# The subtraction that makes the low half of o moves from GpSimd to VectorE, one unit later

## The chip, the cores and the metric

The kernel runs on one core of one Trainium2 chip. The metric is the device time of one execution in microseconds. Engines are TensorE (PE, with PEld for its weight loads), VectorE (DVE), ScalarE (ACT), GpSimd (POOL) and SyncE (SP), which here only issues DMAs. The engines run their own instruction streams in order, and wait for each other on semaphores.

## The reference, cut to what matters

```python
x = x + xattn(layernorm(x), ctx)      # 16 heads of 16, 64 keys a batch, x is 4 x 1024 x 256
x = x + moe(layernorm(x))             # shared expert, and 2 of 8 experts a token

# inside xattn
attn = clip(q @ k.T * scale, -CLAMP, CLAMP)
p = softmax(attn)
o = p @ v                             # 4096 x 256 for all heads
return o @ Wo + bo
```

Products run in float16, each float32 operand as a sum of two halves: high = float16(a), low = float16(a - high). So each product's operands are split first. This holds for the softmax weights p, for o (ahead of the product with Wo) and for the weights of the experts. The change is about the low half of o.

## The kernel before, in words

Stages follow each other: layer norm, queries and row maxima (to about 133 us of the span), the attention units (133.9 to 256.3 us), the shared expert with routing, the experts chosen per token. The change lies in the attention units.

There are `NU` = 16 units of 256 tokens, with indices u = 0 to 15, and a loop (`run_units`) that calls each engine's `unit(u)` for u = 0 to 20. In one call an engine works on several units at once: `known(u, lag)` says whether u - lag is a unit. The text calls the call for u "unit u", and writes v for the unit whose data is worked on. In unit u:

- TensorE makes the scores of unit u in four PSUM banks (24 matmuls); then for r = 0 to 3 it multiplies p of unit u-2 with the values (`weigh`, 12 matmuls) and subtracts the row maximum from bank r (`subtract_max`, 2 matmuls). Last is `project(u - 4)`, o times Wo, 12 matmuls of 256 columns. The next unit's scores wait until ScalarE has taken the exponentials out of the banks.
- VectorE clips each of the four banks (`clip`, line 932), which `subtract_max` of the same r waits for. Then come, for v = u-5, the residual sum (line 969) and the moments of the second layer norm (lines 976, 982), and for v = u-2 `normalise` (lines 939, 947), which divides by the row sum and writes o in float32 (`o_f`). In units 16 to 18 it also splits weights of the shared expert (`split_lo`, line 989).
- ScalarE takes four exponentials (line 757), casts r = 0 to 2 to the high half of p (line 764), casts `o_f` of v = u-2 to the high half of o (line 777, semaphore `oh_ready`), and casts r = 3. In units 16 to 18 it casts weights (`split_hi`, line 750).
- GpSimd makes the low half of p for r = 0 to 3 (line 608), which `weigh` waits for two units later. Ahead of r = 3 it makes the low half of o for v = u-2 (line 601): it waits for `oh_ready`, and for the transposes that read the buffer two units ago (`ot_got`), and raises `ol_ready`.
- SyncE waits for `ol_ready` and issues two DMA transposes per unit (line 452), which `project(v)` waits for (`ot_got`). `project(v)` also waits for the residual sum of v-1, since they share a bank. `normalise(v)` waits for `ol_ready` of v-2, and ScalarE's cast of o for `ot_got` of v-2.

`o_f`, `o_hl` and `o_t` have two buffers each. The order within each engine is the order in which the code is written.

Of the kernel before, what the change touches and what calls it, by code (L numbers as in the profile page):

```python
# [5 lines left out]
ALU = mybir.AluOpType  # L6
# [11 lines left out]
def build(nc, x, ctx_t, wq, bq, wk, bk, wv, bv, wo, bo, gate_t, w_all, out):  # L18
# [15 lines left out]
    UT = 2  # L34
# [29 lines left out]
    with ExitStack() as ctx:  # L64
# [3 lines left out]
        def sem(name):  # L68
            return ctx.enter_context(nc.semaphore(name))
# [45 lines left out]
        def carve(shape, dt, parts=P):  # L115
            n = 1
            for s in shape:
                n *= s
            cols = n * (2 if dt in (F32, I32) else 1)
            a = arena[0:parts, used[0]:used[0] + cols]  # L120
            used[0] += (cols + 15) // 16 * 16
            assert used[0] <= E * 3 * 2 * 1024
            if dt != F16:
                a = a.bitcast(dt)
            if len(shape) == 1:
                return a
            names = "abcde"[:len(shape)]
            return a.rearrange(f"p ({' '.join(names)}) -> p {' '.join(names)}",
                               **{k: v for k, v in zip(names, shape)})
# [54 lines left out]
        o_f = carve([2, UT, C], F32)  # L184
        o_t = carve([2, UT, 2, HF, P], F16)
        used[0] = loads_from
        o_hl = carve([2, UT, 2, C], F16)
# [97 lines left out]
        oh_ready = sem("oh_ready")  # L285
        ol_ready = sem("ol_ready")
        ot_got = [sem("ot_got0"), sem("ot_got1")]
# [104 lines left out]
        def known(u, lag):  # L392

            return 0 <= u - lag < NU
# [103 lines left out]
        def _(pool):  # L498
# [94 lines left out]

            def unit(u):
                for r in range(RT):
                    if r == 3 and known(u, 2):
                        v = u - 2
                        pool.wait_ge(oh_ready, v + 1)
                        if v >= 2:
                            pool.wait_ge(ot_got[v % 2], 16 * UT * (v // 2))  # L600
                        pool.tensor_tensor(o_hl[:, v % 2, :, 1], o_f[:, v % 2], o_hl[:, v % 2, :, 0],  # L601
                                           ALU.subtract).then_inc(ol_ready, 1)
                    if known(u, 0):
                        k = RT * u + r
                        pool.wait_ge(ph_ready, k + 1)
                        if u >= PB:
                            pool.wait_ge(pv_ready, u - PB + 1)
                        pool.tensor_tensor(p_l[:, u % PB, r], p_f[:, k % FB], p_h[:, u % PB, r],  # L608
                                           ALU.subtract).then_inc(pl_ready, 1)

            run_units(unit)


# [240 lines left out]
        def _(dve):  # L854
# [51 lines left out]
            for n in range(NG):  # L906
# [6 lines left out]
                if n == 6:  # L913
                    dve.wait_ge(v_copied, B)
                    link(dve.tensor_copy(v_hh, v_f))
                    for h2 in range(2):
                        r = slice(h2 * KV, (h2 + 1) * KV)
# [11 lines left out]
            def clip(u, r):  # L929
                if known(u, 0):  # L930
                    dve.wait_ge(st_scored, RT * u + r + 1)
                    dve.tensor_scalar(bank[r][:, :], bank[r][:, :], CLIP, -CLIP, ALU.min,
                                      ALU.max).then_inc(st_clipped, 1)

            def normalise(v):

                dve.wait_ge(pv_ready, v + 1)
                for t in range(UT):
                    ins = dve.reciprocal(r_sum[:, t].rearrange("p (j h) -> p j h", h=2),
                                         bank[4 + t][:, 0:HD // 2 * OW].rearrange(  # L940
                                             "p (j w) -> p j w", w=OW)[:, :, 2 * D:OW])
                ins.then_inc(norm_link, 1)
                dve.wait_ge(norm_link, v + 1)
                if v >= 2:
                    dve.wait_ge(ol_ready, v - 1)
                for t in range(UT):
                    ins = dve.tensor_tensor(
                        o_f[:, v % 2, t].rearrange("p (j h d) -> p j h d", j=HD // 2, h=2),
                        bank[4 + t][:, 0:HD // 2 * OW].rearrange("p (j w) -> p j w", w=OW)
                        [:, :, 0:2 * D].rearrange("p j (h d) -> p j h d", h=2),  # L950
                        r_sum[:, t].rearrange("p (j h) -> p j h", h=2).unsqueeze(3)
                        .to_broadcast([P, HD // 2, 2, D]), ALU.mult)
                ins.then_inc(of_ready, 1)
# [9 lines left out]
            def residual(v):  # L963

                dve.wait_ge(y_ready, v + 1)
                if v == 0:
                    dve.wait_ge(bo_added, NG)
                xu = x_sb[:, bass.ts(v, UT), :]
                dve.tensor_tensor(xu, xu, bank[6][:, :].rearrange("p (t c) -> p t c", t=UT),
                                  ALU.add).then_inc(y_added, 1)  # L970

            def moments(v):

                dve.wait_ge(y_added, v + 1)
                for t in range(UT):
                    link2(dve.bn_stats(stats[:, v % 2, t], x_sb[:, UT * v + t, :]), False)

            def mean_and_variance(v):

                dve.wait_ge(ln2_link, UT * (2 * v + 1))  # L980
                for t in range(UT):
                    link2(dve.bn_aggr(mv2[:, UT * v + t], stats[:, v % 2, t]), False)

            def split_lo(q):

                if q % 2 == 0:
                    w = w_sh[:, q] if q < 3 else w_qs[:, q - 3]
                    dve.wait_ge(w_hi, q + 1)
                    dve.tensor_tensor(w[:, 1], w_stage[:, q % 4, :], w[:, 0], ALU.subtract).then_inc(w_lo[q % 4], 1)

            def unit(u):
                for r in range(RT):
                    clip(u, r)
                if known(u, 5):
                    residual(u - 5)
                    moments(u - 5)
                    mean_and_variance(u - 5)
                if known(u, 2):
                    normalise(u - 2)
                if NU <= u < NU + 3:  # L1000
                    split_lo(u - NU)

            run_units(unit)

            dve.wait_ge(ln2_link, 2 * NT)
# [638 lines left out]
```

## Time and profile before

| | us |
|---|---|
| median of 3 runs | 772.41 (771.75 to 775.31) |
| profiled execution, its own time | 772.33 |
| its span | 770.3 |

| engine | busy us | share of the span |
|---|---|---|
| PE | 623.3 | 81% |
| DVE | 453.0 | 59% |
| POOL | 390.4 | 51% |
| ACT | 347.6 | 45% |

Shares are means over stages with different limits. In the attention units from 182.4 to 201.4 us, for instance, PE, DVE, ACT and POOL are each busy over 90% of the time. The granted clock of TensorE is given as a part of full speed: 1.00 is 2.4 GHz, 0.50 is 1.2 GHz, and a number between them is a mean over a stretch that has both. In a timeline row the columns are the start in us from the start of the span, the duration of the group of instructions merged in the row, the engine, the line of the program, the operation, the tiles written and read with their shapes, the count, and in brackets the idle time of the engine before it with what ended it.

### The profile page before, as it was taken

How to read it: one execution, taken by the hardware profiler on the slowest of the kernel's cores; microseconds unless marked ns; L12 is line 12 of the kernel's file. 1: busy time of each engine (PE TensorE's matmuls, PEld its weight loads, DVE VectorE, ACT ScalarE, POOL GpSimd, SP SyncE). 2: the span in 40 equal slices, each digit the busy share in tenths (PEclk: the TensorE clock that was granted, in tenths of full speed). 3: DMA queues.
4: the chain of work that ended last, by engine and by line, in shares of the span. 5: the costliest groups of instructions: out<-in, count | busy, mean ns of one | idle time of the engine just before them, and what ended most of it. 6: DMA issues, size and time to landing. Idle time of an engine off the chain costs nothing.

```text
span 770.3 us, 15425 instructions
## 1 busy us (share of the span) xinstructions
PE 623.3 (81%) x5262; PEld 419.9 (55%) x5262; DVE 453.0 (59%) x908; ACT 347.6 (45%) x565; POOL 390.4 (51%) x326
## 2 busy tenths in 40 slices
PE   4377855799996187765769989999999999999991
PEld 2134322356564144432445557788787787887881
DVE  5963487557797345667986664444444444544541
ACT  3645661778894365642115434333333333433430
POOL 6738491588996011220002634647566666566643
PEclk9877796558897699987989999999999999999996
DMA  8400000021323438663003556655565565685743
GB/s 265 141 2 0 1 1 0 1 43 34 53 41 60 121 81 197 159 215 73 8 1 110 185 177 112 97 84 99 92 112 92 97 104 88 96 103 90 101 63 34
DMA packets 108170, 66.12 MB, mean 86 GB/s; under 512 B 82946, under 2 KB 101316, under 8 KB 108100
## 3 DMA queue, kind: packets, MB, share of 16 engines
q1 hardware_dynamic: 93268, 41.91, 24.3%
q0 software_dynamic: 14832, 23.24, 18.1%
q8 instruction: 48, 0.79, 0.5%
q14 instruction: 22, 0.18, 0.1%
HBM read 29.47 MB, written 17.96 MB: 62 GB/s over the span
## 4 chain that ended last, share of the span: by engine, by line
PE 52%; DVE 17%; POOL 9%; issue 8%; ACT 7%; DMA 4%; SPq 2%; POOLq 0%; ACTq 0%; DVEq 0%
PE bank L1275 50%; POOL arena L608 5%; POOL arena L601 2%; DVE hidden L1210 2%; SPq L462 2%; DMA out<-w_stage,map_i 1%; ACT arena L691 1%; PE bank L1577 1%; DVE arena L866 1%; PE bank L1333 1%; DMA arena<-arena 1%; ACT arena L792 1%; DVE arena L897 1%; DVE arena L1150 1%; DVE hidden L1177 1%
## 5 line engine op out<-in xcount | busy, mean ns | idle before, releaser
L1275 PE MATMUL bank<-arena 128*128 128x34 f16 (+6 forms) x1284 | 140.9, 255 | 39.1 <-DVE arena L1153 8.8
L1275 PE MATMUL bank<-qx,arena 128*128 128x256 f16 (+1 forms) x1584 | 156.8, 285 | 4.0 <-ACT hidden L757 3.1
L632 POOL DMA_INDIRECT out<-w_stage,map_i x71 | 114.0, 1606 | 74.4 <-DMA out<-w_stage,map_i 36.6
L1275 PEld LDWEIGHTS bank<-qx,arena 128*128 (+1 forms) x1584 | 125.8, 101 | 26.3 <-ACT hidden L757 5.0
L1275 PEld LDWEIGHTS bank<-arena 128*128 128x128 f16 (+2 forms) x1284 | 76.1, 108 | 95.6 <-issue 41.5
L645 POOL TENSOR_TENSOR arena<-w_stage,arena 128x1024 f16<-128x1024 f32 x12 | 26.5, 2206 | 165.9 <-ACT arena L750 165.9
L1244 DVE TENSOR_TENSOR hidden<-bank,hidden 128x512 f32<-128x512 f32 x71 | 49.1, 692 | 104.1 <-ACT hidden L835 104.1
L1275 PE MATMUL bank<-arena,qx 128*128 (+1 forms) x316 | 85.3, 394 | 27.5 <-DVE arena L897 24.7
L1275 PE MATMUL bank<-arena,w_stage 128*128 x852 | 104.6, 273 | 0.6 <-DVE w_stage L1263 0.4
L835 ACT ACTIVATE hidden<-bank 128x512 f32<-128x512 f32 x71 | 42.4, 597 | 127.7 <-PE bank L1275 127.7
L619 POOL DMA_INDIRECT qx<-rows_d,map_i x71 | 71.4, 1006 | 48.5 <-DVE lane_w L1236 30.6
L1275 PE MATMUL bank<-qx,w_sh 128*128 128x512 f16 x384 | 93.6, 396 | 0.0
L1275 PEld LDWEIGHTS bank<-arena,w_stage 128*128 128x128 f16 x852 | 82.3, 98 | 16.9 <-issue 2.9
L608 POOL TENSOR_TENSOR arena<-hidden,arena 128x512 f16<-128x512 f32 x64 | 72.4, 1162 | 28.2 <-ACT arena L764 28.2
L1263 DVE TENSOR_TENSOR w_stage<-hidden,w_stage 128x512 f16<-128x512 f32 x71 | 49.3, 694 | 45.1 <-ACT w_stage L847 45.1
L1275 PE MATMUL bank<-w_sh,hidden 128*128 128x256 f16 x384 | 53.7, 296 | 27.0 <-DVE hidden L1210 27.0
L1275 PEld LDWEIGHTS bank<-arena,qx 128*128 128x128 f16 x316 | 31.1, 100 | 69.8 <-issue 42.7
L1275 PEld LDWEIGHTS bank<-qx,w_sh 128*128 128x128 f16 x384 | 39.3, 102 | 43.3 <-issue 7.3
L897 DVE TENSOR_REDUCE arena<-bank 128x8 f32<-128x512 f32 x64 | 42.4, 688 | 34.6 <-PE bank L1275 34.5
L1275 PEld LDWEIGHTS bank<-w_sh,hidden 128*128 128x128 f16 x384 | 38.9, 105 | 41.1 <-DVE hidden L1210 32.8
L847 ACT CAST w_stage<-hidden 128x512 f16<-128x512 f32 x71 | 43.9, 619 | 37.9 <-DVE hidden L1244 35.6
L806 ACT ACTIVATE hidden<-bank 128x512 f32<-128x512 f32 x32 | 19.1, 596 | 81.4 <-PE bank L1275 81.4
(183 smaller groups left out, 758.8 us busy)
## 6 DMA issues: line engine op xcount, KB each, us to landing
w_stage<-in_w_all SPq DMA_DIRECT2D x27, 512.0 KB, 4.6
x_sb<-in_x SPq DMA_DIRECT2D x8, 512.0 KB, 8.0
rows_d<-arena SPq DMA_DIRECT2D x8, 512.0 KB, 3.5
out<-x_sb POOLq DMA_DIRECT2D x8, 512.0 KB, 5.7
qx<-rows_d,map_i POOLq DMA_INDIRECT x71, 2.9
qx<-qx SPq DMA_TRANSPOSE x71, 2.6
out<-w_stage,map_i POOLq DMA_INDIRECT x71, 3.9
arena<-arena SPq DMA_TRANSPOSE x32, 2.5
```

What stands on the lines that cost most here:

```text
L462: sp.dma_start_transpose(qx[:, :, :, bass.ts(GT * g + t, P)].rearrange("p s h t -> p (s h) t"), x2_hl[:, g % XB, t].rearrange("p a c -> p ...
L608: pool.tensor_tensor(p_l[:, u % PB, r], p_f[:, k % FB], p_h[:, u % PB, r], ALU.subtract).then_inc(pl_ready, 1)
L619: pool.indirect_dma_start(out=gathered(r), out_offset=None, in_=rows_d, in_offset=bass.IndirectOffsetOnAxis(ap=map_i[:, 0, i:i + 1], axis= ...
L632: pool.indirect_dma_start(out=out, out_offset=bass.IndirectOffsetOnAxis(ap=map_i[:, 1, i:i + 1], axis=0), in_=y_sb[:, r], in_offset=None, ...
L645: pool.tensor_tensor(w[:, 1], w_stage[:, q % 4, :], w[:, 0], ALU.subtract).then_inc(w_lo[q % 4], 1)
L806: act.activation(act_g[:, hc % 2], bank[hc % 2][:, :], ACT.Silu).then_inc(silu_ready, 1)
L835: act.activation(act_g[:, k % 2], bank[k % 2][:, :], ACT.Silu).then_inc(sp_silu, 1)
L847: act.copy(h_sp[:, k % 3, 0], h_f[:, k % 2]).then_inc(sp_hh, 1)
L897: dve.tensor_reduce(m_raw[:, n % 2, i, bass.ts(hf, HH)], bank[4 + hf][:, :].rearrange("p (h k) -> p h k", h=HH), AX.X, ALU.max).then_inc(s ...
L1244: dve.tensor_tensor(h_f[:, k % 2], bank[2 + k % 2][:, :], act_g[:, k % 2], ALU.mult).then_inc(sp_h, 1)
L1263: dve.tensor_tensor(h_sp[:, k % 3, 1], h_f[:, k % 2], h_sp[:, k % 3, 0], ALU.subtract).then_inc(sp_hl, 1)
L1275: return pe.matmul(o, a, b, start=first, stop=last, skip_group_check=not check)
```

## The change: what it does

GpSimd no longer makes the low half of o. VectorE makes it, in the same form, in unit u for v = u-3, between the clips of r = 1 and r = 2. The waits move with it. In units 16 to 18, which have no clips, it stands ahead of the residual sum.

```diff
--- before.py
+++ after.py
@@ gpsimd: unit(u) @@
                 for r in range(RT):
-                    if r == 3 and known(u, 2):
-                        v = u - 2
-                        pool.wait_ge(oh_ready, v + 1)
-                        if v >= 2:
-                            pool.wait_ge(ot_got[v % 2], 16 * UT * (v // 2))
-                        pool.tensor_tensor(o_hl[:, v % 2, :, 1], o_f[:, v % 2], o_hl[:, v % 2, :, 0],
-                                           ALU.subtract).then_inc(ol_ready, 1)
                     if known(u, 0):
@@ vector @@
+            def split_o(v):
+
+                dve.wait_ge(oh_ready, v + 1)
+                if v >= 2:
+                    dve.wait_ge(ot_got[v % 2], 16 * UT * (v // 2))
+                dve.tensor_tensor(o_hl[:, v % 2, :, 1], o_f[:, v % 2], o_hl[:, v % 2, :, 0],
+                                  ALU.subtract).then_inc(ol_ready, 1)
+
             def unit(u):
                 for r in range(RT):
                     clip(u, r)
+                    if r == 1 and known(u, 3):
+                        split_o(u - 3)
                 if known(u, 5):
                     residual(u - 5)
                     moments(u - 5)
```

## Rows read from the trace of the kernel before

**Rows 1.** The chain of waits, shares by line, from 145 to 236 us.

```profile
by line: POOL arena L608 44.0%; issue 28.5%; POOL arena L601 15.9%; PE bank L1275 5.6%; DMA arena<-arena 4.5%; SPq L452 1.3%; DVE bank L932 0.8%; ACT hidden L757 0.8%; ACT arena L764 0.6%; POOLq L607 0.4%; POOLq L600 0.2%
```

**Rows 2.** Busy time by stretch: length, each engine's busy us, granted clock, DMA.

```profile
182.40:201.40 19.00, 17.72 (x320) 12.08 (x320) 17.66 (x44) 17.80 (x30) 17.84 (x17) 1.00 0.29 44
201.40:211.70 10.30, 9.91 (x110) 5.96 (x112) 7.13 (x22) 8.29 (x16) 8.73 (x9) 0.67 0.39 54
```

**Rows 3.** Timeline of unit 8, all engines, a unit at the full clock.

```profile
187.25 2.49 DVE L932 TENSOR_SCALAR bank<-bank 128x512 f32<-128x512 f32 x4 [0.31 <-PE bank L1275]
...
188.01 3.96 PE L1275 MATMUL bank<-arena 32*128 32x256 f16 x56 [0.38 <-DVE bank L932]
...
188.43 2.84 ACT L757 ACTIVATE hidden<-bank,arena 128x512 f32<-128x512 f32 x4
189.04 0.51 PEld L1275 LDWEIGHTS bank<-arena 128*128 128x128 f16 x14 [0.21 <-issue]
189.65 0.68 DVE L969 TENSOR_TENSOR x_sb<-x_sb,bank 128x512 f32<-128x512 f32 x1
...
189.76 0.51 PEld L1275 LDWEIGHTS bank<-arena 128*128 128x128 f16 x14 [0.21 <-POOL arena L608]
...
191.17 1.65 ACT L764 CAST arena<-hidden 128x512 f16<-128x512 f32 x3
...
191.69 0.76 DVE L947 TENSOR_TENSOR arena<-bank,arena 128x256 f32<-128x256 f32 x2
...
192.72 0.62 ACT L777 CAST arena<-arena 128x512 f16<-128x512 f32 x1
```

**Rows 4.** Timeline of DVE and of POOL: first clips and first subtractions of units 5, 7, 8, 9.

```profile
167.67 2.49 DVE L932 TENSOR_SCALAR bank<-bank 128x512 f32<-128x512 f32 x4 [3.21 <-PE bank L1275]
...
181.75 2.49 DVE L932 TENSOR_SCALAR bank<-bank 128x512 f32<-128x512 f32 x4 [1.81 <-PE bank L1275]
...
192.76 2.49 DVE L932 TENSOR_SCALAR bank<-bank 128x512 f32<-128x512 f32 x4 [0.32 <-PE bank L1275]
...
165.10 3.38 POOL L608 TENSOR_TENSOR arena<-hidden,arena 128x512 f16<-128x512 f32 x3 [0.99 <-ACT arena L764]
...
179.58 3.38 POOL L608 TENSOR_TENSOR arena<-hidden,arena 128x512 f16<-128x512 f32 x3 [1.55 <-ACT arena L764]
...
186.35 3.39 POOL L608 TENSOR_TENSOR arena<-hidden,arena 128x512 f16<-128x512 f32 x3 [1.16 <-ACT arena L764]
```

**Rows 5.** VectorE subtractions of this shape, with GpSimd idle (min/median/max ns) and busy.

```profile
L1263 DVE TENSOR_TENSOR w_stage<-hidden,w_stage x71: 681/693/748, 464.6 to 752.3; 128x512 f16<-128x512 f32 x71
...
298.06 2.12 POOL L645 TENSOR_TENSOR arena<-w_stage,arena 128x1024 f16<-128x1024 f32 x1 [11.54 <-ACT arena L750]
298.53 2.20 DVE L1210 TENSOR_TENSOR hidden<-hidden 128x512 f16<-128x512 f32 x1 [1.57 <-ACT hidden L820]
...
109.05 2.89 POOL L565 TENSOR_TENSOR qx<-arena,qx 128x512 f16<-128x512 f32 x2
109.40 1.52 DVE L912 TENSOR_TENSOR arena<-arena 128x512 f16<-128x512 f32 x1
```

**Rows 6.** Timeline of PEld: the 12 weight loads of `project` at either clock.

```profile
196.07 1.21 PEld L1275 LDWEIGHTS bank<-arena 128*128 128x128 f16 x12 [0.30 <-DMA arena<-arena]
...
201.69 2.26 PEld L1275 LDWEIGHTS bank<-arena 128*128 128x128 f16 x12 [0.33 <-issue]
```

**Rows 7.** Timeline of units 15 to 20, all engines.

```profile
228.97 2.49 DVE L932 TENSOR_SCALAR bank<-bank 128x512 f32<-128x512 f32 x4 [0.32 <-PE bank L1275]
...
238.15 0.62 ACT L777 CAST arena<-arena 128x512 f16<-128x512 f32 x1 [2.57 <-DMA arena<-arena]
...
239.75 1.84 DVE L989 TENSOR_TENSOR w_sh<-w_stage,w_sh 128x1024 f16<-128x1024 f32 x1 [1.97 <-ACT w_sh L750]
...
245.03 1.16 POOL L601 TENSOR_TENSOR arena<-arena 128x512 f16<-128x512 f32 x1 [4.52 <-ACT arena L777]
...
251.60 0.69 DVE L969 TENSOR_TENSOR x_sb<-x_sb,bank 128x512 f32<-128x512 f32 x1 [0.58 <-PE bank L1275]
```

## The prediction

> **What bounds the kernel now.** I read the attention stage in four steps. The chain of waits comes first: from 145 to 236 us it gives GpSimd 60% (line 608 with 44.0%, line 601, the one that moves, with 15.9%) [rows 1]. Taken alone this promises a gain of up to 16 times 1.12 us. The busy times by stretch speak against it: between 182.4 and 201.4 us TensorE, VectorE, ScalarE and GpSimd are busy 17.72, 17.66, 17.80 and 17.84 us of 19.00 [rows 2]. Four engines stand at their limit, and the chain had to choose one.
>
> So I went to the timeline of unit 8 [rows 3], whose first clip starts at 187.25; unit 9's starts at 192.76 [rows 4], a period of 5.51 us. Of it ScalarE uses about 5.45 (exponentials from 188.43, casts from 191.17, o from 192.72), so with GpSimd free the floor is ScalarE's, under 0.1 us away. VectorE waits 0.32 us in the period, ahead of the first clip, and works 5.19. TensorE's loop is the tight one: scores, first clip, first `subtract_max` (188.01), three steps of 0.72 us (189.04 to 189.76 is one), `project`, next scores. GpSimd needs 5 times 1.12 = 5.6 us and drifts behind, but what it makes is used two units later. Removing its line 601 shortens no loop by itself, except the 0.30 us for which `project` waits on late transposes [rows 6].
>
> Last, the clock. It is 1.00 from 182.4 to 201.4 us and 0.67 on the mean in the next 10.3 us [rows 2]: some of that at 1.2 GHz. A `project` at the lower clock takes 2.26 us of weight loads, not 1.21 [rows 6]. Scores behind it are slower too. Units that have this take about 7.1 us instead of 5.5. They can be told by how long ahead of the first clip GpSimd starts on p: 2.57 us in unit 5 (165.10 and 167.67), 2.17 in unit 7, 0.90 in unit 8 [rows 3, 4]. Units 5, 6, 7, 11, 12 are of this slow kind (2.17 to 2.57, mean 2.32), units 8, 9, 10, 13, 14 of the fast kind (0.90 to 0.98).
>
> **The change part by part.**
>
> *Removed from GpSimd:* 16 subtractions of 1.16 us (one in [rows 7]). Worth about 0.3 us in all by the reasoning above, the wait of `project`.
>
> *Added to VectorE:* 16 subtractions of 128x512, two inputs from SBUF. With GpSimd idle this form takes 0.69 us (71 rows, 681 to 748 ns), 0.60 from start to start. With GpSimd at work it takes longer, and the rows show how: one starts at 298.53 while GpSimd's runs from 298.06 to 300.18, and ends at 300.73; it takes 2.20 us. One at 109.40 takes 1.52, and the two GpSimd instructions beside it take 2.89 instead of 2.32 [rows 5]. I read this as turns: VectorE gets nothing until GpSimd's current instruction ends, then runs 0.55 us, and GpSimd's next one waits for it.
>
> Two rules of the Trainium skill bear on this, both on "GPSIMD Engine Reference". Its "Engine selection" sends elementwise work on a tile to VectorE as about twice as fast; its "Specifications" says that GpSimd's SBUF interfaces are shared with VectorE, with contention for instructions with two SBUF inputs. By the first alone an added subtraction would cost 0.60 us and this sum would be that of the first rival below; the trace agrees with it only where GpSimd is idle.
>
> *Where the added instruction falls.* In unit 8 clips start every 0.60 us (187.25 to 189.65 for four [rows 3]), so it would start at 188.45. GpSimd's first three subtractions run from 186.35 to 189.74 [rows 4]; the second ends at 188.62. The added one ends at 189.17, and the third clip starts at 189.08 instead of 188.45: 0.63 us late. TensorE would take the third `subtract_max` at 188.01 + 2 x 0.72 = 189.45; the clip for it was there at 189.21. So 0.24 us is hidden and 0.39 is not. What is behind the instruction on VectorE moves by 0.63: clips 2 and 3, residual, moments, `normalise`. That chain then fills the period, 5.19 + 0.63 = 5.82 against TensorE's 5.90. ScalarE's cast of o starts after `normalise` and still ends about 0.5 us before VectorE wants it, so the moved wait on `oh_ready` costs nothing in units 3 to 15. Five fast units: 5 x 0.39 = 2.0 us.
>
> In a slow unit the first clip comes later against GpSimd's p, and the instruction meets the last of the four. Unit 7: start at 181.75 + 1.20 = 182.95; GpSimd's third ends at 182.96 and its fourth follows at once, until 179.58 + 4.5 = 184.1. The third clip then starts at 184.55, 1.6 us late, 1.36 of it visible. Unit 5: 1.2 late, 0.96 visible. The late clips are 3.78 us less the lead, so the five units lose 5 x (3.78 - 2.32 - 0.24) = 6.1 us. In units 3 and 4 the clock is 0.50, TensorE's steps are about 1.0 us, and the 0.6 us is hidden.
>
> *The end of the stage, units 15 to 20,* in us after the first clip of unit 15 (228.97 [rows 7]). Before, GpSimd lags: ScalarE's cast of o(14) starts at 9.2 because it waits for transposes that line 601 released late. After, these are in time, but VectorE is later. In unit 16 the added instruction needs o(13)'s cast, which ends at 6.5, then a turn behind GpSimd, until 7.8; residual, moments and `normalise` of v=14 end at 10.55, and the cast starts at 10.6, 1.4 late. `split_hi` and `split_lo` follow; the latter took 1.84 us beside GpSimd [rows 7] and now takes 1.2: 0.8 late. The added instruction of v=14 makes it 1.4 late again; that of v=15 takes 0.7 where GpSimd's took 1.2. Residuals and weight splits then queue in order, and the last residual (251.60, 22.6) comes at about 23.8. Cost 1.2 us; bounds -1.5 (the transposes' early arrival decides) and +3.2 (all four added instructions are on the path).
>
> *The clock.* The added wait leaves TensorE idle 0.4 to 1.4 us more in each unit, between the steps. No row shows what that does. Bounds: the falls stop (four of them cost 1.6 us each, and their units no longer pay the larger wait, 1.0 each: about -10 us), or every fast unit becomes slow, 5 x (1.6 + 0.85) = +12. I take one more slow unit, +2.4, as in the rows it is the stretches with the least matmul work that are followed by a fall. "TensorE: Matmul & The Clock Gate" of the Trainium skill, section "HAM oscillation", blames falls on long idle gaps; by it the short ones added here would cost nothing and the term would be 0. The trace doesn't agree: the fall at 201.4 us follows 19 us in which TensorE was busy 93%.
>
> *Sum:* 2.0 + 6.1 + 1.2 - 0.3 + 2.4 = 11.4 us. On the profiled execution's 772.33 us, which is 0.1 from the median of 772.41, that gives 783.7. The stages behind only start later. Bounds of the loop alone: at least 10 x 0.36 = 3.6 (never a turn to wait for), at most 10 x (0.60 + 1.12 - 0.24) = 14.8 (a whole GpSimd instruction each time).
>
> **The rivals.**
>
> *The instruction is not stretched in the loop.* The two turns meet well, and it costs 0.60 us everywhere: 10 x 0.36 + 1.2 - 0.3 = 4.5, 776.8 us. For it: in fast units it is nearly so (0.63), and in units 7 and 12 the start misses the end of GpSimd's third instruction by hundredths. Against it: units 5, 6 and 11 miss it by 0.15 us or more.
>
> *The clock stays up: no slower than before.* If the longer period moves `project` so that the falls of units 5 to 7, 11 and 12 don't happen, ten units take 5.9 us each, 59.0 instead of 61.3 (167.67 to 228.97 [rows 4, 7]). With 1.2 for the end and -0.3 it is 771.0 us. It decides from the point where three or more of the five slow units become fast. For it: units 8 to 10 kept the full clock with 0.38 us idle per unit. Against it: the added wait lowers TensorE's share of work, and unit 5 starts from the lower clock.
>
> *The clock falls in nearly every unit.* Slow units are longer, and so have longer stretches without `project`; the state keeps itself up. All ten slow: 9.0 + 12.3 = 21.3 us, 793.6.
>
> **How the numbers follow.** Changes under 0.5% (3.9 us, so 768.5 to 776.3) can hardly be told from none. Forecast (turns, clock much as before, 777 to 790): 0.62, all slower. Not stretched: 0.12, half of it slower by over 0.5%. Clock stays up: 0.11, 0.07 of it the same and 0.04 faster. Clock falls everywhere: 0.15, slower. Faster 0.04, same 0.13, slower 0.83. The range 774.5 to 793 leaves out the steady clock and the upper half of the last case, 0.18 together. The predicted time is 783.7.
>
> **What would show it.** The trace after must have 16 subtractions on VectorE with GpSimd idle after its fourth p of each unit; those of fast units take about 0.7 us, those of slow ones 1.3 to 1.7, each ending 0.55 us behind the end of a GpSimd instruction. TensorE must wait for the third clip in each unit from 5 on, the period of fast units be 5.9 us, and `project` wait for no transposes. The last residual should come 23.8 us after unit 15's first clip. It is wrong if the added instructions take 0.69 us beside a busy GpSimd, if TensorE's steps don't open up, or if the number of `project` groups at 2.26 us is far from six.

## The result, and the profile after

The changed kernel takes 796.41 us (median; 788.68 to 799.09) where the kernel before takes 773.86 us (771.75 to 775.77). The ratio is 1.0276, with a 95% interval of 1.0195 to 1.0356: slower by 2.8%. The interval lies wholly above 1, though not wholly above 1.02. The prediction was 783.7 us with a range of 774.5 to 793: the sign was right, the loss is twice the 11.4 us forecast, and the time lies above the range. The profiled execution took 794.96 us, with a span of 793.0.

In the changed kernel the lines of GpSimd, ScalarE and VectorE up to `clip` stand 7 lower (608 is now 601, 932 is 925, 969 is 962), the added subtraction is line 989, and the matmul helper 1278.

The chain of waits of the changed kernel, by line, from 145 to 252 us (answers to [rows 1]):

```profile
by line: PE bank L1278 63.2%; DVE bank L925 16.5%; DVE arena L989 11.5%; issue 6.5%; ACT hidden L750 1.3%; DVE x_sb L962 1.1%; DVEq L960 0.0%
```

GpSimd, 60% before, is gone from it. TensorE, the clips and the added subtraction are the chain now: the tie of four engines [rows 2] has become, by this chain, a loop of two.

Busy times by stretch, the kernel before and the changed one (columns as in [rows 2]):

```profile
165.00:235.00 70.00, 65.71 (x1027) 42.95 (x1026) 56.00 (x144) 60.18 (x104) 62.75 (x57) 0.87 0.27 43
```

```profile
165.00:235.00 70.00, 59.72 (x754) 35.23 (x753) 51.92 (x116) 43.46 (x74) 36.52 (x33) 0.68 0.16 32
```

In 70 us TensorE does 754 matmuls instead of 1027, and the granted clock is 0.68 on the mean instead of 0.87. So more of the stretch was run at 1.2 GHz.

Unit 7 of the changed kernel, timeline, with the start of unit 8 (answers to [rows 3, 4]):

```profile
177.95 4.50 POOL L601 TENSOR_TENSOR arena<-hidden,arena 128x512 f16<-128x512 f32 x4 [3.81 <-ACT arena L757]
...
180.26 1.30 DVE L925 TENSOR_SCALAR bank<-bank 128x512 f32<-128x512 f32 x2 [1.67 <-PE bank L1278]
...
181.46 1.53 DVE L989 TENSOR_TENSOR arena<-arena 128x512 f16<-128x512 f32 x1
...
182.92 1.28 DVE L925 TENSOR_SCALAR bank<-bank 128x512 f32<-128x512 f32 x2
183.66 0.13 PEld L1278 LDWEIGHTS bank<-arena 32*128 32x128 f16 x2 [1.25 <-DVE bank L925]
...
185.18 2.26 PEld L1278 LDWEIGHTS bank<-arena 128*128 128x128 f16 x12 [0.41 <-issue]
...
189.35 1.30 DVE L925 TENSOR_SCALAR bank<-bank 128x512 f32<-128x512 f32 x2 [2.45 <-PE bank L1278]
```

GpSimd's fourth subtraction ends at 182.45. The added instruction waits for that from 181.46 and ends 0.54 us behind it. The third clip is 1.46 us late, TensorE's weight loads wait 1.25 for it, then `project` runs at 1.2 GHz (2.26 us of weight loads), and the next scores take longer too (weight loads 0.99 us, from 187.85, instead of 0.56 at 2.4 GHz). The unit takes 9.09 us. The added instructions (minimum, median, maximum in ns):

```profile
L989 DVE TENSOR_TENSOR arena<-arena x16: 682/1052/1620, 150.0 to 266.3; 128x512 f16<-128x512 f32 x16
```

**Where the 22.7 us of span are.** First clips and last residual sums give the sum. From the first clip of unit 5 to that of unit 15 it is 84.91 us (163.25 to 248.16) instead of 61.30: +23.6. From there to the last residual sum it is 25.97 instead of 22.63: +3.3. Behind that it is +0.2, and the first clip of unit 0 came at 131.36 instead of 135.43, with units 0 to 5 0.35 shorter: -4.4. The stage ahead isn't touched by the change, and its length moves from run to run (131.4 to 137.4 us in the profiles below). So the units and their end cost 26.9 us in this pair of profiles; between the medians of the whole kernel it is 22.6. Two profiles are not two kernels, however: e8 below has the same program as the changed kernel in units 0 to 14, and from unit 5 to unit 15 it took 79.93 us, 5 us less.

At the end, the last `project` of the changed kernel and that of the kernel before (answers to [rows 7]):

```profile
271.37 2.72 PE L1278 MATMUL bank<-arena 128*128 128x256 f16 x12 [0.87 <-DVE x_sb L962]
```

```profile
250.09 1.47 PE L1275 MATMUL bank<-arena 128*128 128x256 f16 x12 [2.70 <-DMA arena<-arena]
```

The last residual sum follows at 274.13, where it was at 251.60.

### The profile page after: what moved, and what is told of

The parts are those of the page before. It is cut to its first block, busy times and chain, and to the rows that moved or that the text cites. A ratio compares the mean times of both kernels' runs of the same rounds, so it can differ in the third digit from the quotient of the medians.

```text
span 793.0 us, 15425 instructions
## 1 busy us (share of the span) xinstructions
PE 636.8 (80%) x5262; PEld 424.4 (54%) x5262; DVE 467.9 (59%) x924; ACT 347.3 (44%) x565; POOL 375.3 (47%) x310
## 3 DMA queue, kind: packets, MB, share of 16 engines
q1 hardware_dynamic: 93268, 41.91, 22.6%
## 4 chain that ended last, share of the span: by engine, by line
PE 56%; DVE 21%; ACT 8%; issue 6%; DMA 4%; SPq 2%; POOL 2%; another core or an unknown queue 1%; POOLq 0%; ACTq 0%; DVEq 0%
PE bank L1278 54%; DVE bank L925 2%; DMA out<-w_stage,map_i 2%; DVE hidden L1213 2%; DVE arena L989 2%; SPq L462 2%; ACT arena L684 1%; PE bank L1580 1%; DVE arena L859 1%; PE bank L1336 1%; POOL out L625 1%; ACT arena L785 1%; DVE arena L890 1%; DVE arena L1153 1%
## 5 line engine op out<-in xcount | busy, mean ns | idle before, releaser
L1278 PE MATMUL bank<-arena 128*128 128x34 f16 (+6 forms) x1284 | 152.1, 268 | 47.7 <-DVE bank L925 14.8
L1278 PE MATMUL bank<-qx,arena 128*128 128x256 f16 (+1 forms) x1584 | 160.6, 299 | 4.3 <-ACT hidden L750 3.1
L1278 PEld LDWEIGHTS bank<-qx,arena 128*128 (+1 forms) x1584 | 127.6, 105 | 28.4 <-issue 5.8
L1278 PEld LDWEIGHTS bank<-arena 128*128 128x128 f16 (+2 forms) x1284 | 80.2, 112 | 111.3 <-issue 47.5
L828 ACT ACTIVATE hidden<-bank 128x512 f32<-128x512 f32 x71 | 42.4, 597 | 127.8 <-PE bank L1278 110.0
L925 DVE TENSOR_SCALAR bank<-bank 128x512 f32<-128x512 f32 x64 | 41.0, 690 | 36.2 <-PE bank L1278 36.2
L750 ACT ACTIVATE hidden<-bank,arena 128x512 f32<-128x512 f32 x64 | 43.4, 687 | 42.5 <-PE bank L1278 42.0
```

The costliest lines, as they stand in the source:

```text
L750: act.activation(p_f[:, k % FB], bank[r][:, :], ACT.Exp, scale=exp_scale).then_inc(exp_ready, 1)
L828: act.activation(act_g[:, k % 2], bank[k % 2][:, :], ACT.Silu).then_inc(sp_silu, 1)
L1278: return pe.matmul(o, a, b, start=first, stop=last, skip_group_check=not check)
```

## The experiments

Ratios are to the kernel before, run beside each experiment on the same chip; its median there was 771.52 us beside e1 to e4, 774.47 beside e5 to e8 and 774.14 beside e9 to e11. The changed kernel was timed only in the first set (before: 773.86). So experiments are compared with each other and with the changed kernel by the ratios, and a difference counts as shown where the intervals don't overlap. "Units" is the time from unit 5's first clip to unit 15's in the profile, "clock" the mean granted clock from 165 to 235 us, each from one profiled execution. For e7 that was the longest of its four (794.45 us), for e8 the shortest of its five (790.06).

| kernel | median us | ratio, 95% interval | units us | clock |
|---|---|---|---|---|
| before | 773.86 | 1 | 61.30 | 0.87 |
| changed | 796.41 | 1.0276 (1.0195 to 1.0356) | 84.91 | 0.68 |
| e1 one input from PSUM | 788.55 | 1.0254 (1.0194 to 1.0314) | 79.97 | 0.65 |
| e2 behind the clips | 788.34 | 1.0236 (1.0169 to 1.0303) | 78.18 | 0.68 |
| e3 changed, 8 fillers | 784.0 | 1.0169 (1.0106 to 1.0231) | 66.81 | 0.92 |
| e4 GpSimd relieved only | 769.99 | 0.9991 (0.9959 to 1.0024) | 65.73 | 0.82 |
| e5 before, 4 fillers | 769.24 | 0.9922 (0.989 to 0.9955) | 56.13 | 1.00 |
| e6 behind the moments, 4 fillers | 772.41 | 0.9967 (0.9934 to 1.0001) | 60.85 | 0.98 |
| e7 changed, 4 fillers | 788.0 | 1.0146 (1.0079 to 1.0213) | 77.36 | 0.81 |
| e8 end on GpSimd | 797.37 | 1.028 (1.0219 to 1.034) | 79.93 | 0.76 |
| e9 e7 with input from PSUM | 781.2 | 1.008 (1.004 to 1.0121) | 70.13 | 0.83 |
| e10 before, fillers everywhere | 765.94 | 0.9875 (0.9817 to 0.9932) | 59.70 | 0.93 |
| e11 behind the moments | 781.39 | 1.0072 (1.0039 to 1.0105) | 67.68 | 0.79 |

The theory going in: the loss has two parts, the third clip's delay (VectorE's added work and its turns with GpSimd), and the clock, which falls because of it. The rivals were that VectorE's load alone sets the pace, and that the clock falls for another cause.

**e1: the turns taken away.**

```diff
-                dve.tensor_tensor(o_hl[:, v % 2, :, 1], o_f[:, v % 2], o_hl[:, v % 2, :, 0],
+                dve.tensor_tensor(o_hl[:, v % 2, :, 1],
+                                  bank[7][:, 0:C].unsqueeze(1).to_broadcast([P, UT, C]), o_hl[:, v % 2, :, 0],
                                   ALU.subtract).then_inc(ol_ready, 1)
```

> The changed kernel, but the first input of VectorE's added subtraction is read from an idle PSUM bank instead of o_f, so it has one input from SBUF and not two; place, shape, waits and the other input stay. (What it writes as the low half of o is not o's.) Theory 1 (turns: it waits for GpSimd's running instruction because both want SBUF): the 16 instructions take 0.68 us each instead of 0.68 to 1.62, the third clip is 0.6 us late instead of 1.0 to 1.5, and TensorE's wait for it falls from 0.66-1.23 us to about 0.4. At ten units that is 4 to 6 us less; with more, if the clock falls less often: 777 to 792 us. Theory 2 (the added work on VectorE costs it, whatever GpSimd does): 796, as the changed kernel.

All 16 take 0.68 us now:

```profile
L989 DVE TENSOR_TENSOR arena<-bank,arena x16: 678/680/691, 151.3 to 262.1; 128x512 f16<-128x512 f32 x16
```

With one input from SBUF there is no wait for GpSimd, though GpSimd still runs beside it: this is the clean result. TensorE's matmuls wait 0.29 us for the third clip in six of the ten units and not at all in the others (0.12 to 1.23 in the changed kernel). The median lies within what theory 1 expected, at its upper end, but the ratio of 1.0254 can't be told from the changed kernel's 1.0276, and units of 8.0 us are what e8 took with the turns left in. The clock is no better (0.65, with `project` at 2.26 us in all ten units). So while the clock is down, taking the turns away is not shown to be worth any time.

**e2: behind the clips.**

```diff
-                    if r == 1 and known(u, 3):
+                    if r == 3 and known(u, 3):
                         split_o(u - 3)
```

> The changed kernel, but the added subtraction stands behind the clip of r = 3 instead of r = 1, so no clip waits for it. Theory 1 (the cost arises because TensorE waits for the third clip in the middle of its steps, which also lowers the clock in nearly every unit): TensorE has no wait between its steps, the unit takes 5.8 us at the full clock (VectorE's load) and 7.1 with one project at 1.2 GHz, the number of slow projects falls back towards five of ten; 774 to 782 us. Theory 2 (VectorE's load itself sets the pace, wherever the instruction stands): at least 790.

Neither: 788.34, and the ratio (1.0236) can't be told from the changed kernel's. TensorE's steps had no wait for a clip but the first, and the timeline shows one ahead of `project`, in seven of ten units (0.29 to 1.02 us), that I had not thought of:

```profile
205.96 0.68 DVE L962 TENSOR_TENSOR x_sb<-x_sb,bank 128x512 f32<-128x512 f32 x1
...
206.79 2.72 PE L1278 MATMUL bank<-arena 128*128 128x256 f16 x12 [0.53 <-DVE x_sb L962]
```

`project(u - 4)` waits for the residual sum of u-5, which VectorE makes in the same unit behind the clips, and here behind the added subtraction too (from 205.36). Before, that sum ended at 190.33 us in unit 8 [rows 3] and `project`'s weight loads began at 190.48: there were 0.15 us to spare. e11 below is this kernel with the one instruction moved behind the residual sum and the moments, and its ratio is 1.0072, with no overlap.

**e3: more work for TensorE.**

```diff
                     if known(u, 2):
                         weigh(u - 2, r)
+                    if r == 2 and 3 <= u < NU:
+                        for _ in range(8):
+                            mm(bank[7][:, 0:C], ident[:, :], wo_hl[:, 0, 0], True, True)
```

> The changed kernel with 8 more matmuls of 256 columns in each unit from 3 to 15, into an unused PSUM bank, between weigh and subtract_max of r = 2, where TensorE waits 0.66 to 1.23 us for the third clip. They take 0.86 us at 2.4 GHz and 1.7 at 1.2. Theory 1 (most of the loss is the clock, which falls because a stretch without project holds too little matmul work): more work brings less time. The granted clock stays at 1.00 through most of units 5 to 15, project takes 1.2 us instead of 2.26, a unit 6.3 to 6.8 us instead of 8.5: 775 to 785 us. Theory 2 (the clock doesn't answer to such work): 796 or up to 10 us more.

784.0 us, as theory 1 has it: 104 useless matmuls made the attention units shorter, 66.81 us instead of 84.91 (79.93 in e8). The ratio is 1.0169 against 1.0276, with intervals that overlap by a little. From unit 6 on the period is 6.39 us in every unit, with `project` at 1.21 us; in units 3 and 4, where the fillers ran at 1.2 GHz, they cost time (8.3 and 10.1 us instead of 6.6 and 7.9). Here the added instruction takes 0.71 us, as forecast for a fast unit:

```profile
196.19 4.96 POOL L601 TENSOR_TENSOR arena<-hidden,arena 128x512 f16<-128x512 f32 x4 [1.43 <-ACT arena L757]
...
197.09 1.30 DVE L925 TENSOR_SCALAR bank<-bank 128x512 f32<-128x512 f32 x2 [0.57 <-PE bank L1278]
...
198.30 0.71 DVE L989 TENSOR_TENSOR arena<-arena 128x512 f16<-128x512 f32 x1
```

GpSimd starts 0.90 us ahead of the first clip, and its second subtraction ends 0.16 us after the added one starts: 0.16 and 0.55 make the 0.71.

**e4: GpSimd relieved, nothing added.**

```diff
+                        n = C if v < 2 else 16
-                        pool.tensor_tensor(o_hl[:, v % 2, :, 1], o_f[:, v % 2], o_hl[:, v % 2, :, 0],
-                                           ALU.subtract).then_inc(ol_ready, 1)
+                        pool.tensor_tensor(o_hl[:, v % 2, :, 1, 0:n], o_f[:, v % 2, :, 0:n],
+                                           o_hl[:, v % 2, :, 0, 0:n], ALU.subtract).then_inc(ol_ready, 1)
```

> The kernel before, but from the third on GpSimd's subtraction for o covers 16 of 256 columns per tile (the rest of the low half of o is left as it was), with all its waits and signals; nothing is added to VectorE. It shows what the relief of GpSimd is worth alone. My account (four engines at the limit, GpSimd's products are used two units later): 771 to 773.5 us, at most 2 us gained, from transposes that come in time. The chain of waits taken by its shares (GpSimd is the bound): 14 times 1.0 us less, 759 us.

0.9991, with an interval that holds 1: freeing the engine that the chain names with 60% is worth nothing measurable. (The median is 1 us below the 771 to 773.5 expected, as the kernel before beside it was low too, 771.52.) Its fourteen shortened instructions would have given 14 us by the chain. At the full clock the period is 5.51 with it and without it.

**e5: the clock of the kernel before.** The filler in the kernel before, where TensorE waits for the first clip.

```diff
                         weigh(u - 2, r)
+                    if r == 0 and 5 <= u < NU:
+                        for _ in range(4):
+                            mm(bank[7][:, 0:C], ident[:, :], wo_hl[:, 0, 0], True, True)
```

> The kernel before (GpSimd makes the low half of o) with 4 more matmuls of 256 columns in each unit from 5 to 15, into an unused PSUM bank, between weigh and subtract_max of r = 0, where TensorE waits 0.38 us for the first clip. Theory 1 (a stretch without project holds too little matmul work and the clock falls; more work in it holds the clock): all units from 6 on at 5.5 to 5.7 us, none at 7.0; the four or five slow ones give back 1.5 us each, the added work costs at most 0.1 us a unit: 764 to 769 us, faster than before. Theory 2 (the clock's falls have another cause): 771 to 778.

0.9922, faster than before by 0.8%, with an interval below 1; the median is 0.2 us above the range of theory 1, far closer to it than to theory 2. The clock is 1.00 over the whole stretch and nine of ten periods are 5.50 to 5.83 us, the tenth 6.24; none is 7. The 6.24 and the 5.83 are `project` waiting 0.66 and 0.26 us for its transposes: with the clock held, GpSimd's 5.6 us a unit do show, in two units of ten.

```profile
165.00:235.00 70.00, 65.07 (x1165) 45.13 (x1164) 61.92 (x159) 61.04 (x103) 67.99 (x60) 1.00 0.28 46
```

The fillers fill the 0.39 us in which TensorE waited for the first clip. So they add matmul work and take a wait away at once, and which of the two keeps the clock up was not tried apart. Busy time doesn't tell the two kernels apart (65.07 us of 70 here, 65.71 before).

**e6 and e11: behind the moments, with and without the fillers of e5.**

```diff
                     mean_and_variance(u - 5)
+                if known(u, 3):
+                    split_o(u - 3)
                 if known(u, 2):
```

> The changed kernel with the added subtraction moved behind the moments of v = u-5, so that neither a clip nor the residual sum (which project waits for) stands behind it, and with the 4 filler matmuls at r = 0 in units 5 to 15. It prices VectorE's load with the clock held. Theory 1 (with the clock held and no wait in the steps, the change costs only VectorE's longer round): units of 5.8 to 6.0 us against 5.5, project at 1.2 us throughout; 771 to 777 us. Theory 2 (wait and clock are not what made the changed kernel slow): above 785.

> The kernel of e6 without its fillers: VectorE makes the low half of o behind the moments, nothing holds the clock. With e6 (772) it gives the clock's share alone. Theory 1 (the clock falls more often as soon as the round is longer, and place and clock both matter): VectorE's round 5.7 us, three to eight projects at 2.26 us, units of 7.1 us there: 777 to 785 us. Theory 2 (the place alone is the cure): 772 to 775.

e11 1.0072 and e6 0.9967: the fillers alone are worth 8 to 9 us here, the place (e11 against the changed kernel) about 15. Both differences are clear of the noise, and they are the firmest figures of this document. Place and fillers together take the whole loss away. Both medians lie in theory 1's ranges. In e6 seven of ten units take 5.71 to 5.74 us (the others 6.45, 6.46 and 7.89: in each `project` waits 0.59 to 0.69 us for transposes, which start later from this place, and in the last the clock fell too); e11 has eight of ten units at 6.9 to 7.1 us. In both the added instruction takes 0.66 us in the median, as GpSimd is idle at that point in nearly every unit. With the clock held and the right place, moving the work costs 0.2 us in such a unit (5.51 in e5). Against the kernel before that is no loss that can be told from none; against e5 it is about 3 us, at the edge of the noise.

**e7 and e9: the turns at the full clock.** e7 is the changed kernel with fewer fillers than e3, and from unit 6 on. The edit is shown against e3's. e9 is e7 with the input of e1, and its fillers go to unused columns of bank 4.

```diff
-                    if r == 2 and 3 <= u < NU:      # e3
-                        for _ in range(8):
+                    if r == 2 and 6 <= u < NU:      # e7, e9
+                        for _ in range(4):
-                            mm(bank[7][:, 0:C], ident[:, :], wo_hl[:, 0, 0], True, True)            # e7
+                            mm(bank[4][:, 272:512], ident[:, :], wo_hl[:, 0, 0, 0:240], True, True) # e9
```

> The changed kernel with 4 instead of 8 filler matmuls before subtract_max of r = 2, in units 6 to 15 instead of 3 to 15. With the clock held the wait for the third clip is only 0.4 us, so 4 fillers (0.43 us) fit and the unit should take 5.9 to 6.0 us instead of 6.39. Theory 1: clock up from unit 7 or 8 on, 775 to 780 us, faster than with 8 fillers. If 4 are too few to hold it: units of 8 to 8.5 us and 790 to 798 us.

> The kernel of e7 (4 fillers at r = 2 in units 6 to 15) with the added subtraction's first input from an idle PSUM bank, as in e1 (what it writes as the low half of o is not o's), and the fillers into unused columns of another bank. In e7's units at the full clock the added instruction still took 1.60 us and the unit 7.01. Theory 1 (that is the turn with GpSimd): the instruction takes 0.68 us, at the full clock the unit takes 5.9 to 6.1 us, about 1 us less than e7's in each of ten units; 774 to 782 us. Theory 2 (7.01 us is the price of the place between the clips, or of the residual sum that project waits for): 6.8 to 7.1 us a unit, 788.

e7 missed its expectation (788.0, not 775 to 780), and shows what was missing. Unit 9 and the next one's first clip:

```profile
201.71 4.95 POOL L601 TENSOR_TENSOR arena<-hidden,arena 128x512 f16<-128x512 f32 x4 [3.63 <-ACT arena L757]
...
202.84 1.30 DVE L925 TENSOR_SCALAR bank<-bank 128x512 f32<-128x512 f32 x2 [0.30 <-PE bank L1278]
...
204.04 1.60 DVE L989 TENSOR_TENSOR arena<-arena 128x512 f16<-128x512 f32 x1
...
207.59 1.47 PE L1278 MATMUL bank<-arena 128*128 128x256 f16 x12 [0.17 <-DVE x_sb L962]
...
209.85 1.30 DVE L925 TENSOR_SCALAR bank<-bank 128x512 f32<-128x512 f32 x2 [0.29 <-PE bank L1278]
```

The clock is up (1.22 us of weight loads, from 207.56), and still the unit takes 7.01 us, in five units in a row. GpSimd starts 1.13 us ahead of the first clip, not 0.90. So its second subtraction is over at 203.99, 0.05 us too early, the third has begun, and the added one waits for all of it. e9 takes that away: all 16 take 0.68 to 0.69 us again, and a unit at the full clock takes 6.08 us. Only four of its ten units are at the full clock; the others take 7.4 to 8.3 us. The ratios of e7 and e9 (1.0146 and 1.008) overlap; the 0.93 us is the units' difference.

**e8: the end of the stage.** For v = 13 to 15 GpSimd makes the low half of o at the old place.

```diff
+                    if r == 3 and known(u, 2) and u - 2 >= NU - 3:
+                        v = u - 2
+                        ...
+                        pool.tensor_tensor(o_hl[:, v % 2, :, 1], o_f[:, v % 2], o_hl[:, v % 2, :, 0],
+                                           ALU.subtract).then_inc(ol_ready, 1)
```

> The changed kernel, but for the last three units (v = 13 to 15) GpSimd makes the low half of o at the old place. Theory 1 (in units 16 to 18 the added subtraction stands ahead of the residual sum, which projects, second splits and the second layer norm wait for in a row): the last residual sum comes 22.5 to 24.5 us after the first clip of unit 15, instead of 25.97; 1.5 to 3.5 us less, 793 to 795. Theory 2 (the end is later only because projects ran at 1.2 GHz there): 25.5 to 26.5 us, 796.

The last residual sum comes 24.41 us after unit 15's first clip (268.76 - 244.35), within theory 1's 22.5 to 24.5, at its end. That doesn't show theory 1, however: e2 and e1, with the added instructions in these units where the changed kernel has them, took 24.45 and 24.73, and the kernel before and e5, which have the same program from unit 16 on, 22.63 and 24.05. The end differs by more than the 1.6 us from one profile to the next. The total shows nothing of it either (797.37): 1.6 us is less than the changed kernel's runs differ by (10 us).

Its other units answer a question that e7 left open. Up to unit 14 this is the changed kernel, without a filler, and two of its units, 5 and 11, kept the full clock. Unit 5:

```profile
162.46 4.95 POOL L607 TENSOR_TENSOR arena<-hidden,arena 128x512 f16<-128x512 f32 x4 [1.61 <-ACT arena L763]
...
164.42 1.30 DVE L931 TENSOR_SCALAR bank<-bank 128x512 f32<-128x512 f32 x2 [2.61 <-PE bank L1284]
...
165.62 0.77 DVE L995 TENSOR_TENSOR arena<-arena 128x512 f16<-128x512 f32 x1
...
167.06 1.10 PE L1284 MATMUL bank<-arena 32*128 32x256 f16 x16 [0.38 <-DVE bank L931]
...
168.33 1.47 PE L1284 MATMUL bank<-arena 128*128 128x256 f16 x12 [0.17 <-DVE x_sb L968]
```

The lead is 1.96 us, the added instruction meets the end of GpSimd's third and takes 0.77, and TensorE waits 0.38 us for the third clip and 0.17 for the residual sum. The unit takes 6.17 us, unit 11 with a lead of 1.93 takes 6.21. So 7.01 is not what a unit of the changed kernel at the full clock must take.

**e10: a faster kernel.** The kernel before with e5's fillers in every unit, and more of them ahead of and in the first units.

```diff
                 if known(u, 4):
                     project(u - 4)
+                elif u < 4:
+                    for _ in range(12):
+                        mm(bank[7][:, 0:C], ident[:, :], wo_hl[:, 0, 0], True, True)
@@ row_scores(n, some), behind each product @@
+                    if n == NG - 1 and j >= 1:
+                        pe.wait_ge(v_copied, B)
+                        for _ in range(4):
+                            mm(bank[7][:, 0:C], ident[:, :], wq_hl[:, 0, 0], True, True)
```

> The kernel before with filler matmuls of 256 columns in all places where the clock fell or hadn't risen: 4 behind each of the last 7 score products of the row maxima (TensorE waits about 1 us there), 4 at r = 0 in all units (as in e5), and 12 in place of the missing project in units 0 to 3. GpSimd makes the low half of o. Theory 1 (more matmul work, less time): clock 1.00 from unit 0 or 1 on, units 2 and 3 in 5.5 us instead of 6.6, unit 4 in 5.5 instead of 7.7 to 8.4: about 4 us less than e5, 761 to 767 us. Theory 2 (the fillers at 1.2 GHz stand in the way as in units 3 to 5 of e3): 769 to 776 us.

0.9875, faster than the kernel before and the changed one; from e5's 0.9922 it can't be told apart. Units 2 to 4 take 5.5 us instead of 6.6, 6.6 and 8.2. Unit 0 takes 7.25, and in two units the clock still fell (7.71 and 7.58 us), so more matmuls do not hold it everywhere, and this is not the end of it. In both units `project` had waited for its transposes, 0.57 and 0.64 us; e5's unit with such a wait (0.66) kept the clock.

## Why the prediction was wrong

*Relief of GpSimd, -0.3 us.* Right in size: e4 shows no gain that can be told from none.

*The turns.* Right as a mechanism, and close in size. The forecast's duration is the end of the running GpSimd instruction plus 0.55 us: for leads of 2.79, 2.31 and 2.53 us that is 1.06, 1.54 and 1.32 us, and units 6, 7 and 9 show 1.05, 1.53 and 1.32. By the lead of the unit the price goes up and down (0.71 at 0.90 in e3, 1.60 at 1.13 in e7, 0.77 at 1.96 in e8). e1 and e9 take the wait away by changing nothing but where one input lies. The rule of "Engine selection" in the Trainium skill's "GPSIMD Engine Reference" holds for the instruction alone (0.69 us against 1.16); in ten units beside GpSimd it took 1.05 to 1.62, which is the sharing that its "Specifications" names.

*Five fast units at 0.39 us, 2.0 us.* There was no fast unit left: all ten had `project` at 2.2 to 2.3 us. And at the full clock the price isn't 0.39. In e8's two fast units it is 0.66 and 0.70 us: the wait for the third clip is the forecast's (0.38 and 0.42), but the forecast put `project`'s wait for the residual sum at nothing, and that adds 0.17. With a lead of 1.13 it is 1.50 (e7). The step also took the lead of [rows 3, 4] as fixed, since everything behind the third clip moves together; e3, e7 and e8 have three leads in the same program but for the fillers. That the residual sum's wait makes the longer lead is a guess; it was not tried alone. How much it matters that the instruction stands ahead of the residual sum is shown by e2 against e11: 1.0236 against 1.0072.

*Slow units, 6.1 us for five.* A slow unit of the changed kernel takes 8.49 us on the mean, about 8.3 by the forecast's terms (7.1 + 1.2). The count of five was off: it went by the lead, and unit 7, its example, with a lead of 2.17, took 5.50 us (181.75 to 187.25 [rows 3, 4]). Only four units, 5, 6, 10 and 11, had `project` at 1.2 GHz and took 7.0 to 7.1. The lead says what the turn costs, not what the clock is.

*The clock, +2.4 us.* This is the step that failed. I took one more slow unit; it was six more, ten `project` groups at 1.2 GHz instead of four (eight in e8), and the prediction's own sign of being wrong, a number far from six, came. The rival "the clock falls in nearly every unit" gave 793.6 us and was given 0.15. By the units' lengths the 2.36 us that a unit lost (8.49 - 6.13) fall into four parts. VectorE's added work in this place is 0.57 (e9's 6.08 less e5's 5.51). The turns are 0.93 if a unit of the changed kernel at the full clock takes e7's 7.01, and 0.11 if it takes e8's 6.19. The clock in the changed kernel is then 1.48 or 2.30 (8.49 less 7.01 or 6.19), against 0.62 in the one before (6.13 less 5.51). Ten times that is 5.7 + 9.3 + 8.6 = 23.6 us, or 5.7 + 1.1 + 16.8 = 23.6. The forecast for the same was 8.1 for the first two and 2.4 for the clock. So the clock's term was too small by 6 to 14 us in either reading; whether the first two were too small as well (15.0) or not (6.8) stays open.

That more matmuls in TensorE's waits keep the granted clock up is shown by e3, e5 and e6: 0.92 instead of 0.68, 1.00 instead of 0.87, and 0.98 instead of 0.79 in e11. What it is in the longer unit that brings the clock down, the missing work or the waits themselves, stays open. By the long idle gaps of "HAM oscillation", in the Trainium skill's "TensorE: Matmul & The Clock Gate", the clock should not have answered to waits of 1.2 us, the longest of the matmuls between 165 and 235 us; the trace of the changed kernel doesn't agree, with TensorE busy 59.72 of these 70 us and the granted clock at 1.2 GHz for most of them (0.68 on the mean). The measurement decides, as it did in the prediction, where I gave it too little weight.

*The end, +1.2 us.* It was 3.3, just outside the bounds of -1.5 and +3.2. The residual sum of v = 13 was already 2.7 us late (18.79 us after unit 15's first clip instead of 16.12). The last two projects ran at 1.2 GHz (2.72 us each instead of 1.47), but the kernel before lost 2.70 us there in a wait for transposes. What the added instructions' place makes of it is not shown: with the same program from unit 16 on the end came at 22.63 (before) and 24.05 (e5).

## What to carry to other kernels

In a stage where four engines are each above 90% busy the chain of waits names one of them, and freeing it was worth nothing here. What the receiving engine does next, and who waits for it (a clip, but also a residual sum that frees a bank), was the cost. Price a VectorE instruction with two inputs from SBUF by GpSimd's instruction that runs when it starts, and put it where GpSimd is idle and nobody waits behind it: that alone took the ratio from 1.0276 to 1.0072. Where the granted clock is between its levels in the kernel before, a wait added to TensorE's loop can cost more in clock than in waiting, so give that term a wide range. A few useless matmuls in a wait gained 0.8% here; they cost time where the clock is down.

## What the runs showed of the hardware

- VectorE waits for GpSimd's running instruction to end when its own has two inputs from SBUF, and ends 0.55 us behind it. The same instruction takes 0.68 us when one of these comes from PSUM, beside a busy GpSimd (e1, e9). Missing the end of GpSimd's instruction by 0.05 us costs 0.9 us (0.71 in e3, 1.60 in e7).
- The granted clock fell to 1.2 GHz in all ten units of the changed kernel with TensorE busy 85% of the time. Four more matmuls of 256 columns a unit (0.60 us in the profile, pipelined with others) raised it from 0.87 on the mean to 1.00 in the kernel before (e5), for a gain of 5 us, with TensorE busy 93% of the time in one and 94% in the other. With the same fillers and more it still fell in two units (e10).
- Runs of one kernel differ by more than four of them tell: the kernel before spread by 0.5% in its first four (771.75 to 775.77), and by 1.3 to 1.9% in each of the later sets of 13 to 23 (765.75 to 779.92 beside e1). Two profiles of the same program, the changed kernel's and e8's, differ by 5 us in ten units.
